# Layer kernel on one core: the gate's root per group of tiles, one masking operation, fewer choosing operations

## What is computed

```python
qkv = layernorm(h) @ W_qkv + b_qkv                 # q, k, v
pq, pk = elu(q) + 1, elu(k) + 1
kv = einsum('bshd,bshm->bhmd', pk, v)
z = 1 / (einsum('bshd,bhd->bsh', pq, pk.sum(axis=1)) + 1e-6)
h = h + einsum('bshd,bhmd,bsh->bshm', pq, kv, z)    # called h2 below
x2 = layernorm(h)                                   # divides by sqrt(v + 1e-5)
logits = (x2 / sqrt(sum(x2 * x2) + 1e-12)) @ (sim / norm(sim)) - sigmoid(gates)
_, top_idx = top_k(logits, 2)                       # the two experts of a token
```

## Time and profile before

| | |
|---|---|
| three runs | 1060.51, 1060.92, 1061.6 us; median 1060.92 |
| profiled execution, span | 1060.5 us |
| first stage | up to about 389 us of the span |
| PE, DVE, POOL busy over the span | 964.6 us, 872.8 us, 680.9 us |
| DVE busy in the first stage, 50 to 250 us | 187.21 us of 200 |

### The profile page before, as it was taken

One profiled execution on the slowest core, in us unless ns is written; L12 is line 12 of the kernel. 1 busy time (PEld: TensorE's weight loads), 2 busy tenths in 40 slices (PEclk: granted clock), 3 DMA queues, 4 the chain that ended last, 5 costly groups with the idle time before them and its releaser, 6 DMA issues.

```text
span 1060.5 us, 23609 instructions
## 1 busy us (share of the span) xinstructions
PE 964.6 (91%) x6830; PEld 889.4 (84%) x6830; DVE 872.8 (82%) x2884; ACT 581.5 (55%) x1569; POOL 680.9 (64%) x896
## 2 busy tenths in 40 slices
PE   4999999999999639999999599999999999999998
PEld 3778887887788528999999499999999999998997
DVE  4799999999999747555555399999999999999998
ACT  4666666666666305444444355655555556555554
POOL 5447777777776683000000588888888888888885
PEclk9999999999999859999999699999999999999999
DMA  2123344443333257888886332333333233333231
GB/s 65 52 72 125 122 143 150 150 135 123 124 124 101 95 189 233 285 277 256 254 266 226 111 90 87 100 97 90 90 100 98 85 93 100 84 93 100 83 93 36
DMA packets 106308, 137.72 MB, mean 130 GB/s; under 512 B 13762, under 2 KB 93634, under 8 KB 106180
## 3 DMA queue, kind: packets, MB, share of 16 engines
q1 hardware_dynamic: 87348, 83.98, 25.2%
q0 software_dynamic: 17408, 50.35, 16.1%
q10 hardware_dynamic: 1424, 1.84, 0.5%
HBM read 70.06 MB, written 66.06 MB: 128 GB/s over the span
## 4 chain that ended last, share of the span: by engine, by line
DVE 44%; PE 36%; issue 10%; POOL 5%; ACT 2%; DMA 2%; SPq 1%; POOLq 0%; DVEq 0%; ACTq 0%
PE bank L1383 10%; PE bank L1385 9%; PE bank L1384 9%; DVE w_attn L1366 6%; DVE x L1320 4%; DVE qk_e L1320 4%; PE bank L1390 4%; DVE phi L1072 3%; DVE row_x L1360 3%; DVE attn L1084 2%; DVE kvm L1105 2%; POOL sorted_x L694 2%; DVE stats L1112 2%; DVE stats L957 2%; DVE zden L1081 1%
## 5 line engine op out<-in xcount | busy, mean ns | idle before, releaser
L1383 PE MATMUL bank<-wo_hi,split_lo 128*128 128x256 f32 x1024 | 304.8, 298 | 9.9 <-DVE x L1320 4.4
L1385 PE MATMUL bank<-wo_hi,split_hi 128*128 128x256 f32 x1024 | 289.0, 282 | 0.0
L1384 PE MATMUL bank<-wo_lo,split_hi 128*128 128x256 f32 x1024 | 288.7, 282 | 0.0
L1383 PEld LDWEIGHTS bank<-wo_hi,split_lo 128*128 128x128 f32 x1024 | 194.1, 190 | 23.1 <-DVE x L1320 11.3
L1384 PEld LDWEIGHTS bank<-wo_lo,split_hi 128*128 128x128 f32 x1024 | 194.3, 190 | 0.0
L1385 PEld LDWEIGHTS bank<-wo_hi,split_hi 128*128 128x128 f32 x1024 | 193.7, 189 | 0.0
L890 ACT ACTIVATE h<-bank,rwo 128x256 f32<-128x256 f32 x256 | 107.3, 470 | 117.9 <-PE bank L1385 113.9
L767 POOL DMA_INDIRECT row_y<-sorted_y,pair_now x128 | 124.2, 970 | 31.8 <-issue 18.3
L760 POOL COPY pair_now<-pair_at 128x2 uint32<-128x2 uint32 x64 | 16.0, 249 | 178.3 <-SPq L567 178.3
L1221 DVE TENSOR_TENSOR split_lo<-bank,split_hi 128x256 fp32r<-128x256 f32 x144 | 61.0, 424 | 69.1 <-ACT split_hi L852 67.8
L1320 DVE SCALAR_TENSOR_TENSOR x<-bank,rwo,x 128x256 f32<-128x256 f32 x256 | 108.5, 473 | 2.2 <-PE bank L1385 1.8
(11 more groups left out here) (215 smaller groups left out, 2630.5 us busy)
## 6 DMA issues: line engine op xcount, KB each, us to landing
sorted_y<-row_y SPq DMA_DIRECT2D x36, 384.0 KB, 3.2
sorted_y<-w_attn SPq DMA_DIRECT2D x36, 384.0 KB, 3.1
row_x<-sorted_x SPq DMA_DIRECT2D x72, 128.0 KB, 2.9
h_rows<-h SPq DMA_DIRECT2D x64, 128.0 KB, 1.7
row_x<-h_rows SPq DMA_DIRECT2D x64, 128.0 KB, 2.3
out_h<-row_x SPq DMA_DIRECT2D x64, 128.0 KB, 1.7
phi<-sorted_x SPq DMA_DIRECT2D x36, 128.0 KB, 3.0
qk_neg<-sorted_x SPq DMA_DIRECT2D x36, 128.0 KB, 3.1
```

The lines of the kernel that those rows point to most:

```text
L1383: pe.matmul(ps, left[1][c], right[0][c], start=(c == 0), stop=False)
L1384: pe.matmul(ps, left[0][c], right[1][c], start=False, stop=False)
L1385: last = pe.matmul(ps, left[0][c], right[0][c], start=False, stop=(c == n - 1))
```

## The change

In each tile DVE masks the state and its sums in one operation over 2 x 136 columns instead of two (2 x 128 and 2 x 8). For this the ones behind v are 8 columns wide instead of 2, so PE's state product (L1464) has 136 columns instead of 130. `roots_in` and POOL's root have two values a row instead of three.

The gate's root is formed per group: in the choosing step DVE forms `root_sq` and `energy_in` right behind `centers` and ahead of `weight_lo` and `phi`, and POOL takes the power -0.5 of 4 (or 2) values right behind `roots` and ahead of the gather and the scatters. `experts_chosen` waits for the result and loses two operations. The two comparisons with the expert numbers are one of 128 columns, and so are the two products and the two sums of `rows_placed`; the last of them writes the whole number directly, without a copy. POOL converts the positions once at the start of the second stage.

```diff
@@ POOL step1
-                    pool.tensor_tensor(roots[:, row, :], roots_in[:, row, :], minus_half[:, 0:3], ALU.pow
+                    pool.tensor_tensor(roots[:, row, :], roots_in[:, row, :], minus_half[:, 0:2], ALU.pow
                                        ).then_inc(done["roots"], 1)
+                g = group_at(i.c)
+                if g is not None:
+                    n = GROUPS[g][1]
+                    quad_done(pool, "gate_scaled", g - 1)
+                    quad_done(pool, "energy_in", g)
+                    pool.tensor_tensor(energy[:, 0:n], energy_in[:, 0:n], minus_half[:, 0:n], ALU.pow
+                                       ).then_inc(done["energy"], 1)
@@ POOL sorted_way
+                pool.tensor_copy(rows, position_u[:, :, :].rearrange("p b n -> p (b n)")).then_inc(pairs_placed, 1)
+                pool.wait_ge(pairs_placed, 1)
@@ DVE
+            def energy_formed(g):
...
+                dve.tensor_tensor(root_sq[:, 0:n], roots[:, rows, 1], roots[:, rows, 1], ALU.mult
+                                  ).then_inc(gate_own, gate_count("root_sq"))
+                gate_wait("root_sq")
+                dve.scalar_tensor_tensor(energy_in[:, 0:n], moments[:, rows, 1, 1], LN_EPS * NORM_EPS / C,
+                                         root_sq[:, 0:n], ALU.add, ALU.mult).then_inc(done["energy_in"], 1)
@@ DVE experts_chosen
-                dve.tensor_tensor(energy[:, 0:n], roots[:, rows, 2], roots[:, rows, 1], ALU.mult
-                                  ).then_inc(gate_own, gate_count("energy_part"))
-                gate_wait("energy_part")
-                dve.tensor_tensor(energy[:, 0:n], energy[:, 0:n], roots_in[:, rows, 1], ALU.mult
-                                  ).then_inc(gate_own, gate_count("energy"))
-                gate_wait("energy")
+                quad_done(dve, "energy", g)
@@ DVE experts_numbered
-                dve.tensor_tensor(is_one[:, 0:n, :], numbers, top_at[:, tiles, 0:1].broadcast_to([P, n, E]),
-                                  ALU.is_equal)
-                dve.tensor_tensor(is_two[:, 0:n, :], numbers, top_at[:, tiles, 1:2].broadcast_to([P, n, E]),
-                                  ALU.is_equal).then_inc(gate_own, gate_count(f"is_two {g}"))
+                dve.tensor_tensor(is_pick[:, :, 0:n, :],
+                                  expert_no[:, :].unsqueeze(1).unsqueeze(1).broadcast_to([P, 2, n, E]),
...
@@ DVE rows_placed
-                dve.tensor_tensor(picked[:, 0, 0:n, :], ranks[:, 0:n, :], is_one[:, 0:n, :], ALU.mult
...
-                dve.tensor_tensor(picked[:, 1, 0:n, :], ranks[:, 0:n, :], is_two[:, 0:n, :], ALU.mult
...
-                dve.tensor_reduce(pair_in_x[:, tiles, 0], picked[:, 0, 0:n, :], AX_X, ALU.add)
...
-                dve.tensor_copy(position_u[:, tiles, :], pair_in_x[:, tiles, :]).then_inc(done["position_index"], 1)
+                dve.tensor_tensor(picked[:, :, 0:n, :], is_pick[:, :, 0:n, :],
+                                  ranks[:, 0:n, :].unsqueeze(1).broadcast_to([P, 2, n, E]), ALU.mult
...
+                    dve.tensor_reduce(position_u[:, tiles, :].rearrange("p t k -> p k t"), picked[:, :, 0:n, :], AX_X,
+                                      ALU.add).then_inc(done["position_index"], 1)
@@ DVE step1
+                g = group_at(i.c)
+                if g is not None:
+                    energy_formed(g)
...
-                    dve.tensor_tensor(kvm[:, :, 0:P], ps_kv[:, :, 0:P],
-                                      head_mask[:, :].unsqueeze(1).broadcast_to([P, G, P]), ALU.mult)
-                    dve.tensor_tensor(kvm[:, :, P:NUMW], ps_kv[:, :, P:P + 1].broadcast_to([P, G, HG]),
-                                      head_of_row[:, :].unsqueeze(1).broadcast_to([P, G, HG]), ALU.mult
+                    dve.tensor_tensor(kvm[:, :, :], ps_kv,
+                                      kv_mask[:, :].unsqueeze(1).broadcast_to([P, G, NUMW]), ALU.mult
...
-                    dve.tensor_scalar(roots_in[:, row, 0:2], moments[:, row, :, 1], LN_EPS, None, ALU.add)
-                    dve.tensor_scalar(roots_in[:, row, 2:3], moments[:, row, 1, 1:2], LN_EPS * NORM_EPS / C, None,
-                                      ALU.add).then_inc(done["roots_in"], 1)
+                    dve.tensor_scalar(roots_in[:, row, :], moments[:, row, :, 1], LN_EPS, None, ALU.add
+                                      ).then_inc(done["roots_in"], 1)
```

More of the change, by code:

```diff
@@ L54 @@
             "attn", "h2", "x2_normed", "x2_turned", "x2_T", "logits_product"]
-GATE_STEPS = ["gate_scaled", "earlier_rows", "rank_product", "ranks", "position_index"]
+GATE_STEPS = ["energy_in", "energy", "gate_scaled", "earlier_rows", "rank_product", "ranks", "position_index"]
 P2_STEPS = ["pair_turned", "pair_hi", "pair_lo", "pair_product", "pair_copied"]
@@ L146, in build @@
         causal, earlier = x1T[:, 0:P], x1T[:, P:2 * P]
-        head_mask = sb("head_mask", [P, P])
-        head_of_row = sb("head_of_row", [P, HG])
+        kv_mask = sb("kv_mask", [P, NUMW])
+        head_mask, head_of_row = kv_mask[:, 0:P], kv_mask[:, P:NUMW]
         ones = sb("ones", [P, P])
@@ L181, in build @@
         moments = sb("moments", [P, N_ROOTS, 2, 2])
-        roots_in = sb("roots_in", [P, N_ROOTS, 3])
-        roots = sb("roots", [P, N_ROOTS, 3])
+        roots_in = sb("roots_in", [P, N_ROOTS, 2])
+        roots = sb("roots", [P, N_ROOTS, 2])
         centers = sb("centers", [P, N_ROOTS, 2])
@@ L199, in build @@
         energy = sb("energy", [P, QUAD])
-        is_one = sb("is_one", [P, QUAD, E])
-        is_two = sb("is_two", [P, QUAD, E])
+        energy_in = sb("energy_in", [P, QUAD])
+        root_sq = sb("root_sq", [P, QUAD])
+        is_pick = sb("is_pick", [P, 2, QUAD, E])
         top_two = sb("top_two", [P, QUAD, E], F32R)
@@ L972, in gate_wait @@
                 dve.wait_ge(gate_own, gate_at[what])
+            def energy_formed(g):
+                first, n = GROUPS[g]
+                rows = slice(first + 3, first + 3 + n)
+                quad_done(dve, "energy", g - 1)
+                dve.tensor_tensor(root_sq[:, 0:n], roots[:, rows, 1], roots[:, rows, 1], ALU.mult
[3 more added lines that the diff above has]
+                                         root_sq[:, 0:n], ALU.add, ALU.mult).then_inc(done["energy_in"], 1)
             def experts_chosen(g):
@@ L977, in experts_chosen @@
                 tiles = slice(first, first + n)
-                rows = slice(first + 3, first + 3 + n)
                 ps = ps_logits[g % 2][:, 0:n, :]
                 after(dve, "logits_product", Tile(first + n - 1))
-                dve.tensor_tensor(energy[:, 0:n], roots[:, rows, 2], roots[:, rows, 1], ALU.mult
-                                  ).then_inc(gate_own, gate_count("energy_part"))
-                gate_wait("energy_part")
-                dve.tensor_tensor(energy[:, 0:n], energy[:, 0:n], roots_in[:, rows, 1], ALU.mult
-                                  ).then_inc(gate_own, gate_count("energy"))
-                gate_wait("energy")
+                quad_done(dve, "energy", g)
                 dve.tensor_tensor(scaled[:, 0:n, :], ps, over_experts(energy[:, 0:n], n), ALU.mult
@@ L1006, in experts_numbered @@
                 quad_done(dve, "position_index", g - 1)
[L1007 to L1011 removed]
+                dve.tensor_tensor(is_pick[:, :, 0:n, :],
+                                  expert_no[:, :].unsqueeze(1).unsqueeze(1).broadcast_to([P, 2, n, E]),
+                                  top_at[:, tiles, 0:2].rearrange("p t k -> p k t").unsqueeze(3).broadcast_to(
+                                      [P, 2, n, E]), ALU.is_equal).then_inc(gate_own, gate_count(f"is_pick {g}"))
             def rows_counted(g):
@@ L1039, in rows_placed @@
                 quad_done(dve, "ranks", g)
-                dve.tensor_tensor(picked[:, 0, 0:n, :], ranks[:, 0:n, :], is_one[:, 0:n, :], ALU.mult
-                                  ).then_inc(gate_own, gate_count("place_one"))
-                dve.tensor_tensor(picked[:, 1, 0:n, :], ranks[:, 0:n, :], is_two[:, 0:n, :], ALU.mult
-                                  ).then_inc(gate_own, gate_count("place_two"))
-                gate_wait("place_one")
-                dve.tensor_reduce(pair_in_x[:, tiles, 0], picked[:, 0, 0:n, :], AX_X, ALU.add)
-                gate_wait("place_two")
-                dve.tensor_reduce(pair_in_x[:, tiles, 1], picked[:, 1, 0:n, :], AX_X, ALU.add
-                                  ).then_inc(gate_own, gate_count("position"))
-                gate_wait("position")
-                dve.tensor_copy(position_u[:, tiles, :], pair_in_x[:, tiles, :]).then_inc(done["position_index"], 1)
+                dve.tensor_tensor(picked[:, :, 0:n, :], is_pick[:, :, 0:n, :],
+                                  ranks[:, 0:n, :].unsqueeze(1).broadcast_to([P, 2, n, E]), ALU.mult
+                                  ).then_inc(gate_own, gate_count("placed"))
+                gate_wait("placed")
```

(3 more changed lines are left out.)

22 lines of the change are left out of this document (10 added, 12 removed).

## The result

The changed kernel takes 1066.78 us (four runs, 1066.32 to 1067.93) against 1060.72 us (four runs) of the kernel before: 6.06 us more, a ratio of 1.0055 with an interval from 1.0043 to 1.0067. The forecast was 1067.5 us, slower.

A forecast was written before the change was run, and what follows sets the result against it. Bound: a 5.26 us loop through ACT and PE, DVE 0.34 us a group above it, POOL from step 59. Terms +4.2 - 0.4 + 3.0 = 6.8, taken as 6.6: span 1067.1, median 1067.5 us; range 1061.8 to 1071.0.

The forecast's parts named there:

- The loop of 5.26 us: First stage: a second loop through ACT and PE, 5.26 us a step, that work taken from DVE does not shorten.
- Relief of DVE: Middle of first stage: DVE holds 0.34 us a group above the loop, all that its relief can give.
- If the others stay at 5.31: Sign of being wrong: steps other than choosing steps stay at 5.31 us, so DVE was not what held them.
- The choosing step: Steps 7 to 55: POOL's root ahead of gather and scatters delays the next `centers`; 5.9 us instead of 5.26.
- -0.4 ahead of the scatters: Steps three to seven, before scatters begin, come down to the loop: 21.47 to 21.04 us, -0.4.
- The columns: PE's state product: 136 columns instead of 130, about 0.02 us a tile, costed at nothing behind 0.27 us of idle.
- The tail: Choosing steps 59, 61, 63, where POOL is the bound: +0.7, +1.0 and +1.2 to 1.3 us, together +3.0.
- the second stage waits for the last scatter: End of first stage: the second stage waits for the last of POOL's scatters; the tail's +3.0 us entered the sum.
- The rule weighed: POOL's powers: by the skill, two, three or four values cost the same 0.88 us; time 1068.5; the rows were preferred.
- (a): Rival, chance 0.10: POOL not last in the choosing step, middle gains 0.34 us a group; 1057 to 1059 us.
- (b): Rival, chance 0.12: POOL's path binds for about half; middle 0 to +1, tail +1.5; 1061 to 1063 us.
- (c): Rival, chance 0.09: DVE holds up POOL's new root, up to 0.3 us a choosing step, +3.9; 1071.4 us.

The follow-up runs named there:

- the best kernel: Changed kernel with the group's root between the two scatters, and roots and roots_in declared three columns wide, two used: 1054.01 us, ratio 0.9920.

## Why the prediction held, point by point

**What bounds.** The loop of 5.26 us is nearly there: with the root out of the way four steps took 5.28 each. Relief of DVE was put at 0.34 us a group; the best kernel got 0.28. In the changed kernel itself only the placing step became shorter (5.34 to 5.28); the numbering step stayed at 5.33 (5.32 before) and the third at 5.28. The three together take 15.89 us, where 15.78 was forecast and 15.93 was measured before. "If the others stay at 5.31" was the prediction's own sign of being wrong, and at 5.30 on average they nearly did.

**The choosing step.** Forecast 5.9 us, measured 5.79. From `centers` to the next `centers` 6.25 was forecast, and it is 6.20 (200.27 to 206.47); the durations of POOL's powers (1.05 for 1.04, 0.73), the lost wait for `h2` and the wait of `centers` are there one by one, and so are its gaps, but for the one in front of the next root (0.03 instead of 0.13). A group was put at 21.7 and is 21.68, since 0.1 too much in this step and 0.1 too little in the three others cancel. The -0.4 ahead of the scatters is -0.37 (21.47 to 21.10). The sum up to step 55 was +3.4 and is +3.46, and that is nearer than it should be: the twelve groups gave 3.53 where their unrounded terms (5.89 + 15.78 - 21.38 = 0.29 each) give 3.5 and the prediction wrote 3.8, and the measured sum holds the 0.30 of the late start.

**The columns** cost nothing, as the idle time behind that product said. The four products of a tile are 0.02 us longer together, as estimated (31.9 and 32.7 us busy in 51 tiles).

**The tail.** From `phi` of step 55 on, +0.4 and +3.0 less a little were forecast, +3.2, and the last scatter came +3.14. By steps: the first scatters of 59, 61 and 63 came 4.60, 5.32 and 6.70 us later than before. Step 61 was put too high (0.7 measured, 1.0 forecast), step 63 a little too low (1.4 measured, 1.2 to 1.3 forecast), and in steps 60 and 61 the shorter roots gave what was said.

**What failed** is the sentence that the second stage waits for the last scatter, taken as if a delay there passed on in full. It waits for the scatter's rows to land, and a scatter that is issued behind the fills lands sooner after its issue, by 2 us. The +6.6 of the sum is the last scatter's +6.60, of which 4.49 reach the second stage. The 1.6 us that bring the median back near the forecast lie behind that point; the places of the tiles, of which the prediction said nothing, are the one cause of that size found there. So its figure is nearer than its reasons deserve, and that is luck: two terms were missing, and they nearly cancel.

**The rule weighed.** By the figure of the Trainium skill's GPSIMD Engine Reference, section 3.1, for a two-input operation, powers of two and four values would cost the same. Here two took 0.72, three 0.88, four 1.05, eight 1.67 and sixteen 2.89 us; the trace disagrees for this operation.

**The rivals.** (a) needed POOL not to be last: it is last twelve times of twelve. It is what happens when the root stands between the scatters. (b) fell with it; one of POOL's gaps did shrink, by 0.10 us. Its price is also off: a middle of 0 to +1 and a tail of +1.5 give 1062.4 to 1063.4, not 1061 to 1063. (c), DVE holding up the new root, costs at most 0.05 us: the power starts at 200.84, under the split of a weight that runs to 201.02, and takes 1.05 us, where with `energy_in` a step ahead it starts under no such operation and takes 1.00. But its mechanism is real, at another place (below).

## What to carry to other kernels

When work is put on an engine with time to spare, look at what its next customer is queued behind. POOL had 0.99 us of waiting in the choosing step and got 1.05 us of work, yet the work was put ahead of the transfers, and the wait it could have filled stood behind the first scatter. And when a tile changes its size, time the same change with the old size kept: the gain or loss may be the addresses'.

## What the runs showed of the hardware

**An indirect DMA issue on GpSimd is longer when it starts under either of two VectorE operations with 256 values a row and two inputs in SBUF.** From 80 to 330 us of the changed kernel the issues that started while the split of a weight or the sum `h2` ran took 1.24 to 1.26 us, 11 of 11; of the 127 others none took over 1.03. In the twelve other kernels and the one before, 95 of 102 such issues took 1.24 to 1.32 us, and of the rest none over 1.05. The rows of one such pair:

```profile
206.55 0.42 DVE L499 TENSOR_TENSOR wq_lo<-raw,wq_hi 128x256 fp32r<-128x256 f32 x1
```
```profile
206.62 1.24 POOL L616 DMA_INDIRECT row_x<-in_embed_table,ids  x1 [0.19 <-issue]
```

In three of the seven exceptions no more than 0.12 us of the operation was left; in the other four the issue started less than 0.01 us behind the start of VectorE's operation, and that operation took 0.46 us instead of 0.39 (sum) or 0.42 (split). The Trainium skill, SBUF — State Buffer, section "SBUF: two separate sides", says that the two engines share a pair of ports which one of them locks for an instruction, a VectorE operation with two SBUF inputs too. The rows agree as to who waits, the one that comes second; the issue above was 0.21 us longer, while 0.35 us of the split were left.

**A power on GpSimd costs 0.155 us for each value of a row**, on 0.42 us: the five sizes above lie on that line to 0.02, and single groups of them (two values of `energy` in 0.69, four in 1.00) to 0.04.

**TensorE's clock fell behind a late step, but not behind each.** With every fourth step at 6.4 us, at whose end PE stood idle for 1.45 to 1.50 us, the granted clock went from 1.00 to 0.5 (2.4 to 1.2 GHz) four times in twelve, for some 3.4 us each. With every fourth step at 5.79 us (idle 0.83 to 0.87) or 5.96 (1.03 to 1.14) it stayed at 1.00.

**The place of tiles in SBUF moves a stage that the change does not touch** by 3 to 4 us of 460, with the same instructions: 462.0 to 458.8 and 462.9 to 458.9.
